# A graph network block on one core: node table first, no barrier at the first pass, one radial piece ahead of the loop and eight inside it, three one-hot buffers

## The reference

```python
x_j = x[src]
v_j = x_j[:, :384].reshape(E, 128, 3)
s_j = silu(x_j[:, 384:] @ W1 + b1) @ W3 + b3
rbf = jnp.sqrt(2.0 / R_CUT) * jnp.sin(n * jnp.pi * r / R_CUT) / r          # n = 1..20
cutoff = 0.5 * (jnp.cos(jnp.pi * r / R_CUT) + 1.0) * (r < R_CUT)
edge_basis = rbf * cutoff @ W2 + b2
s1, s2, s3 = split(s_j * edge_basis)                                        # 128 columns each
v_msg = v_j * s1[:, :, None] + s3[:, :, None] * edge_attr1[:, None, :]
x = x + segment_sum(concatenate([v_msg, s2]), dst)
```

## Time and profile before

| | before |
|---|---|
| device time, three runs | 711.1, 714.84 (median), 719.67 us |
| span of the profiled execution | 711.8 us |
| busy: PE / DVE / ACT / POOL | 505.8 / 537.0 / 389.5 / 370.2 us |
| first gather issued | 144.38 us |
| first and last product of the loop | 154.72 us, 551.50 us (its end) |
| bytes moved by DMA | 139.26 MB, of these 102.91 by gathers |

### The profile page before, as it was taken

The page is one execution under the profiler, slowest core; times in us unless marked ns, Lnnn a source line. Parts: engine busy times, 40 slices in busy tenths (PEclk is TensorE's granted clock), DMA queues, the critical chain, the costliest instruction groups (busy, mean ns, idle before and its releaser), DMA issues.

```text
span 711.8 us, 13058 instructions
## 1 busy us (share of the span) xinstructions
PE 505.8 (71%) x4260; PEld 234.1 (33%) x4269; DVE 537.0 (75%) x1192; ACT 389.5 (55%) x713; POOL 370.2 (52%) x375
## 2 busy tenths in 40 slices
PE   0276430038888888888888888888888286689996
PEld 0232110013333333334433333333333153344443
DVE  8868861029999999999999999999999443354283
ACT  1054331046777777776776777777776364343200
POOL 5004440067777777777777777777773131025300
PEclk9975555559999999999999999999999688689999
DMA  8413777699888888898888888888884400000021
GB/s 277 166 21 99 199 229 222 183 256 306 269 269 272 269 275 270 267 275 268 269 273 269 270 271 271 270 270 269 273 271 149 160 3 0 1 0 1 2 89 56
DMA packets 54193, 139.26 MB, mean 196 GB/s; under 512 B 10366, under 2 KB 21850, under 8 KB 54124
## 3 DMA queue, kind: packets, MB, share of 16 engines
q0 software_dynamic: 25120, 102.91, 46.3%
q1 hardware_dynamic: 23132, 25.80, 12.8%
q10 hardware_dynamic: 5872, 9.68, 4.1%
HBM read 120.47 MB, written 17.54 MB: 194 GB/s over the span
## 4 chain that ended last, share of the span: by engine, by line
DVE 39%; PE 35%; DMA 8%; issue 8%; ACT 3%; SPq 2%; POOL 2%; DVEq 1%; ACTq 1%; POOLq 0%
PE psum L1192 11%; DVE side L929 10%; PE psum L1282 9%; DVE hot L920 5%; DMA part_rows<-side 5%; DVE side L926 4%; PE psum L1157 4%; DVE work L929 3%; DVE work L947 3%; PE psum L1186 3%; PE psum L1251 3%; DVE hot L911 2%; SPq L358 2%; DVE side L916 2%; DMA side<-node_table,src_c 2%
## 5 line engine op out<-in xcount | busy, mean ns | idle before, releaser
L486 POOL DMA_INDIRECT side<-node_table,src_c x234 | 224.4, 959 | 71.3 <-issue 60.4
L604 ACT ACTIVATE side<-key_no,less_key 128x320 bf16<-128x320 f32 x314 | 159.3, 557 | 30.7 <-SPq L384 28.9
L612 ACT ACTIVATE side<-side,one_f 128x640 bf16<-128x640 bf16 x157 | 128.1, 816 | 10.0 <-PE psum L1168 10.0
L1157 PE MATMUL psum<-w2s,radial 123*128 123x384 bf16 x314 | 78.7, 333 | 66.3 <-DVE side L929 43.5
L1186 PE MATMUL psum<-side,hot 128*32 128x512 f32 x468 | 123.1, 605 | 0.5 <-DVE side L929 0.5
L929 DVE TENSOR_TENSOR side<-side,psum 128x768 f32<-128x768 f32 x117 | 110.5, 945 | 0.0
L486 POOL DMA_INDIRECT work<-node_table,src_c x80 | 76.8, 960 | 60.6 <-SPq L384 36.5
L1192 PE MATMUL psum<-side,hot 128*32 128x128 f32 x1404 | 99.4, 277 | 0.0
L926 DVE TENSOR_TENSOR side<-side,psum 128x512 f32<-128x512 f32 x117 | 79.4, 678 | 1.3 <-DMA side<-node_table,src_c 1.3
L1168 PE MATMUL psum<-side 128*128 128x320 bf16 x314 | 70.3, 306 | 0.5 <-ACT side L612 0.5
L1192 PEld LDWEIGHTS psum<-side,hot 128*32 128x32 f32 x1404 | 68.0, 109 | 0.1
(11 more groups left out here) (202 smaller groups left out, 738.0 us busy)
## 6 DMA issues: line engine op xcount, KB each, us to landing
radial<-part_rows SPq DMA_DIRECT2D x36, 270.0 KB
part_rows<-side SPq DMA_DIRECT2D x6, 810.0 KB, 12.7
side<-node_table,src_c POOLq DMA_INDIRECT x234, 4.2
sum_rows<-stage SPq DMA_DIRECT2D x212, 16.0 KB
node_table<-work ACTq DMA_DIRECT2D x10, 320.0 KB, 7.6
sum_rows<-zeros_bf SPq DMA_DIRECT2D x1, 2688.0 KB, 18.8
side<-sum_rows ACTq DMA_DIRECT2D x10, 256.0 KB, 4.7
xw<-in_x ACTq DMA_DIRECT2D x1, 2304.0 KB
```

The costliest lines, as they stand in the source:

```text
L486: g.indirect_dma_start(out=rows[i % SLOT_PAIRS][:, j, :], out_offset=None, in_=node_table, in_offset=bass.IndirectOffsetOnAxis(ap=src_c[:, ...
L604: a.activation(key_off[:, b, j, :], key_no[:, :], ACT.Abs, bias=less_key[:, t:t + 1]).then_inc(L["key_off_made"], 1)
L612: a.activation(key_hot[:, b, :, :], key_off[:, b, :, :], ACT.Relu, bias=one_f[:, :], scale=-1.0).then_inc(L["key_hot_made"], 1)
L1157: last = mm(bank[2 * (i % 2) + j][:, 0:C3], radial[0:RROWS + 3, t * P:(t + 1) * P], w2s[:, :], start=True, stop=True)
```

## The change

1. *Order of the head.* The last quarter of x is loaded first, into a tile `x_in` in `side`; then W1, W3, the rest of x, the zeros for the sums, all on ACT's queue. `filter_of` starts as soon as `hT` is there; it has three PSUM banks, and the table's rows four buffers instead of two. The edge tables are made between the filters. DVE takes the first filter straight from PSUM. Splitting W2 and the biases, constants and the zeroing of the counts are POOL's; edge numbers to floats and `ea_c` are ACT's. `wu2` shares the buffer of `w3` and is loaded after the last filter.
2. *Radial pieces.* Nine pieces of 120x768, one in the head, eight in the loop: piece 1 at pairs 0 to 8, piece `i` from pair `18 * (i - 1) - 8` on. r and the coefficient are kept in float32 and loaded by SP broadcast over 20 rows; `pick` and its matmuls are gone. The steps lie between the pairs of DVE and ACT. The subtractions that POOL did are DVE's. There is one buffer of everything, and it lies in `xw`, so x is loaded there near the loop's end.
3. *Stacks from SBUF.* `part_rows` is gone: SP copies the parts within SBUF into `radial`, and loads r and the coefficient of the next piece behind them.
4. *No barrier.* Each engine enters the first pass when what it needs itself is there. The pass's close is done only if a second pass follows. Semaphores are counted by constants instead of registers.
5. `HOTS` is 3.

The core of the diff:

```diff
-HOTS = 2
+HOTS = 3
-PIECES = 6
-PB = 3
+PIECES = 9
+FILTER_BANKS = 3
+TABLES = 4
...
+        def rc_piece(k, i):
+            piece = rc_rows[k, i * PG:(i + 1) * PG].rearrange("(c f) -> c f", c=CHUNKS)
+            return piece.unsqueeze(0).to_broadcast((N_RBF, CHUNKS, PC))
+
+        def piece_at(i):
+
+            return 0 if i == 1 else PIECE_PAIRS * (i - 1) - 8
+
+        def piece_pairs(step):
+
+            return {piece_at(i) + step: i for i in range(1, PIECES)}
+
+        def stores_before(i):
+
+            return -(-(piece_at(i) + 2) // GP)
...
+            def load_r(i):
+                if i:
+                    sp.wait_ge(S["turn_begun"], i)
+                sp.dma_start(r_in, rc_piece(0, i)).then_inc(S["r_loaded"], 16)
...
+            def load_stack(i):
+                sp.wait_ge(S["lo_made"], i + 1)
+                for q, k in enumerate(STACK):
+                    sp.dma_start(radial[q * N_RBF:(q + 1) * N_RBF, i * PG:(i + 1) * PG].rearrange("p (c f) -> p c f", c=CHUNKS),
+                                 part[:, k, :]).then_inc(stack_in[i], 16)
...
-            sp.sem_inc(S["pass_go"], 1)
-            with sp.Fori(0, rounds_of(sp)) as r:
...
+                    if n in pieces:
+                        load_stack(pieces[n])
+                        if pieces[n] + 1 < PIECES:
+                            load_r(pieces[n] + 1)
+                            load_coef(pieces[n] + 1)
+                    if pieces and n == NG - 4:
+                        load_x()
+
+            store_sums({stores_before(i): i for i in range(1, PIECES)})
...
+            pool.wait_ge(S["edges_taken"], 3)
+            for b in range(TABLES):
+                pool.wait_ge(table_stored[b], 16 * through(NW, b, TABLES))
+            for i in range(PAIRS):
+                gather(i)
...
+            act.wait_ge(S["x_pads"], 1)
+            load_x(C3, D, S["ld_s"])
+            for to, from_ in ((w1[:, :], W1), (b1c[:, :], b1.rearrange("(p a) -> p a", a=1)), (w3[:, :], W3)):
+                a.dma_start(to, from_).then_inc(S["ld_table_weights"], 16)
+            load_x(0, C3, S["ld_v"])
+            act.wait_ge(S["dve_const"], 2)
+            a.dma_start(sum_rows.rearrange("(p b r) c -> p b (r c)", p=P, b=ZB),
+                        zeros_bf[:, :].bitcast(F32).unsqueeze(1).to_broadcast((P, ZB, 256))).then_inc(S["sums_zeroed"], 16)
...
+            sine_at, high_at, middle_at = piece_pairs(3), piece_pairs(5), piece_pairs(7)
...
+            def turns(i):
+                dve.wait_ge(S["r_loaded"], 16 * (i + 1))
+                if i:
+                    dve.wait_ge(S["lo_made"], i)
+                v.tensor_scalar(wave, r_in, harmonic[:, :], None, ALU.mult).then_inc(S["turn_begun"], 1)
+                dve.wait_ge(S["turn_begun"], i + 1)
+                v.tensor_scalar(nearest, wave, MAGIC, MAGIC, ALU.add, ALU.subtract).then_inc(S["turn_near"], 1)
...
+            turns_at, remainder_at, scaled_at = piece_pairs(0), piece_pairs(1), piece_pairs(4)
+            less_high_at, low_at = piece_pairs(6), piece_pairs(8)
...
+            pe.wait_ge(S["table_vec_made"], NW)
+            pe.wait_ge(S["base_taken"], 1)
+            pe.wait_ge(S["bias_rows_set"], 16)
+            pe.wait_ge(S["carry_zeroed"], 1)
+            pe.wait_ge(S["uv_set"], 1)
+            sum_pass()
```

More of the change, by code:

```diff
@@ L362, in _ @@
[L362 to L372 removed]
+            load_stack(0)
@@ new lines, in _ @@
+            then(g.tensor_scalar(lane_k, lane_k, -float(SPAN), None, ALU.mult))
+            then(g.tensor_tensor(lane, lane, lane_k, ALU.add))
+            then(g.tensor_scalar(lane_diff[:, :], node_no[:, 0:SPAN], lane, -1.0, ALU.subtract, ALU.mult))
+            g.tensor_scalar(stack[:, :], lane_diff[:, :], 0.0, None, ALU.is_equal).then_inc(S["pool_const"], 1)
+            pool.wait_ge(S["edges_turned"], 5)
+            pool.wait_ge(S["span_made"], 2)
+            pool.wait_ge(S["r_stored"], 16)
```

713 lines of the change are left out of this document (349 added, 364 removed).

## The result

The changed kernel took **748.2 us** (median of four runs, 744.9 to 757.3) where the kernel before took 715.2 (median of four, 711.1 to 719.7): 1.043 of the time before, 95% interval 1.036 to 1.051. The ratio leaves out the longest execution, 757.3 us, which fell in the chip's slower state. I had forecast 655, in a range of 637 to 680. It is slower by 4% where I had forecast faster.

What follows compares the result with a forecast made beforehand. The prediction took DVE to bound the loop, with DMA close behind. Start 63, loop 427.3 and tail 161.3 summed to 651.6 us; as the median was 3.0 above the profiled run, it forecast 655, range 637 to 680.

Steps and rivals of the forecast that it cites:

- the sum stores behind a piece come late by less than two groups: 0: Loop, SP's queue: the stage holds sum stores delayed behind a piece's transfers, and SP's issues have room; 0 us.
- not faster: Loop rival: every piece's copies come late, pieces 3 to 8 hold DVE as piece 2 does; 721 us, chance 0.04.
- Third buffer, -16.5: Loop: with three one-hot buffers DVE's L911 no longer waits for the pair two back; -16.5 us.
- Pieces' DVE work, +36: Loop: eight radial pieces add 4.5 us each to DVE, in full on the path; +36 us.
- Blocking: Loop rival: DVE's tensor_scalar and POOL exclude each other, 16 instructions at +1.04 us; 672 us, chance 0.07.
- r late at piece 2, +8: Loop, pair 10: DVE waits 3 to 15 us for piece 2's r, issued behind the stack; +8 us.
- Collisions, +3: Loop, DMA: pieces' copies, gathers and sum stores collide at times while DVE stays the bound; +3 us.
- the ten engines, 671: Loop rival, the second case: ten DMA engines become the bound, +17 in place of +3; 671 us, chance 0.21.
- The loop's sum: First product to end of the last: 396.8 - 16.5 + 36 + 8 + 3 = 427.3 us.
- The start, 63: Head: first product at 63 us instead of 154.7, with hT at 18 and base_b taken at 47.3.
- Stack 0 by 59: hidden: Head: stack 0's six copies issue and land by 59 us, beside the chain to the first product.
- Tail, 161.3: From the last product to the end: 160.3 us as before, +1 for the load of x.

Runs made afterwards that it cites:

- e15: The kernel before with three one-hot buffers and one of six gathers left out from pair 8 on: 697.1 us, 0.979 of before.
- e10: The base with two one-hot buffers instead of three: 698.9 us, 0.977 of before.
- e9: The base run a second time, the same kernel as e4: 684.7 us, 0.957 of before.
- e1: The kernel before with a third one-hot buffer, two tiles cut to make room: 725.9 us, 1.013 of before.
- the base: The changed kernel with the loop pieces' transfers issued from ACT's queue instead of SP's: 686.1 us (e4) and 684.7 us (e9).
- e4: The changed kernel with the loop pieces' transfers on ACT's queue instead of SP's, first run: 686.1 us, 0.957 of before.
- e2: The changed kernel without the 64 transfers of the loop's pieces, their computing steps kept: 682.0 us, 0.953 of before.
- e7: The base with the copy of ones cut in two, 54 packets ahead of stack 0 and the rest behind: 0.916 of before, on another chip.
- e5: The base with two one-hot buffers, on another chip: 0.932 of before.
- e8: The kernel before with the same two tiles cut as in e1 but two one-hot buffers, on another chip: 1.0015 of before.
- e6: The base with the gathers held until stack 0 has landed, on another chip: 0.913 of before.

## Why the forecast was wrong

- **SP's queue, "the sum stores behind a piece come late by less than two groups: 0".** This step failed. Moving the transfers off that queue gives 62 us by time, 66.3 in the loop of the profiled runs, and is enough to make the kernel 4% faster than before. Some 50 of the 66 are this term, forecast at 0; some 16 are the stop for r, forecast at 8. I had the bytes and their own rate (10 us), and took SP's waits of 128 us as room in its queue. But a sum store landed behind what was issued ahead of it on its queue, and that took 27 us where gathers filled the same engines. The stores took 18 to 26 us; `stage` covers 7 to 9. The rival "not faster", at 721, had the right kind (a stop at every piece from 2 on, the clock falling, as it did to 0.50 here), but the wrong waiter: r for the next piece, for which 22 us stand ready, where the stores have 7. I gave it 0.04.
- **Third buffer, -16.5.** Near in size where POOL has room (e15: -20); that e10 against e9 gives -14 is partly luck, as two thirds of the waits it takes away are of another kind. I took before's loop for DVE's alone; it was also the gathers', 7.5 of 7.56 us. "More isn't there since DVE then never stops" is false in e1, where DVE stands 27.7 us for gathers.
- **Pieces' DVE work, +36.** Right: the tensor_scalars took 0.62 and 0.56 us, the four tensor_tensor 0.94 to 0.95, 0.87 from start to start, 4.6 in sum (forecast 4.5). "Blocking" with tensor_scalar over 1 us did not come in the loop; the one of piece 0, at 33.1 us in the head, took 1.36.
- **r late at piece 2, +8.** In after DVE stood 17.2 us for it; three later stops of 1.8 to 3.3 us fall under the waits for sum stores. In the base it isn't among the waits.
- **Collisions, +3, and the ten engines, 671.** The transfers cost 3 to 4 us by time and 3.2 and 0.8 in the loop (e4 and e9 against e2). The second case did not happen.
- **The loop's sum.** The base's loop, without the queue's fault, took 429.6 us where 427.3 were forecast. That is luck in part: the 8 for r were not needed, and something in no term, most likely the long gathers, took their place. With no transfers at all (e2) the loop took 428.8, where the terms without 8 and 3 say 416.3.
- **The start, 63.** The chain to base_b is right to 0.1 us, but by luck: hT was ready at 13.5 us and not 18, since nothing held ACT, and then PE waited 7.21 us for `bias_parts`, which no term had. "Stack 0 by 59: hidden" failed: PE had it at 87.3, for I had left the copy of ones out of the count, though it stands right ahead of the stack on the queue.
- **Tail, 161.3.** 164.2: behind the load of x the last sum stores are 3 us later than I had allowed.

## What to carry to other kernels

Before a bulk transfer is put on a queue, list what is issued behind it there and how long each of these can wait; price the wait by the time the bulk takes beside the other queues' traffic, not by its bytes alone. A small transfer that someone waits for belongs on another queue than a bulk one that nobody needs soon: the same bytes cost 65 us on one and 3 to 4 on the other (15 when spread over the first). And an engine that issues software gathers is full when its issues are back to back; add the gaps to its busy time before calling another engine the bound.

## What the runs showed of the hardware that I had not expected

- Issuing a gather of 128 rows holds POOL 0.95 us and the next starts 0.30 later; when it starts under DVE's SBUF-only tensor_tensors, it takes up to 1.61 (e1). In before, where the two engines have almost the same pace, 1 of 268 gathers starts there; with one wait of DVE taken away it is 66 of 253.
- Issuing a transfer is not of fixed cost. A stack copy took from 0.76 us (e7) to 8.48 (the first behind the ones), a weight load 32.80 behind 432 packets for three engines. The issuing engine stands meanwhile, with all that is behind it.
- A copy into 3 rows ran at a share of 0.16 and 30 GB/s. The Trainium skill (DMA: Bandwidth & Descriptors, section "Why a DMA increments its semaphore by 16 and not by 1") gives it three engines, 0.19; the row agrees.
- The four runs e5 to e8 were on a chip on which the kernel before takes 801 us, 12% more, with the clock at 0.99 and the DMA share lower, 0.77 (e8, 172 to 300 us). Its gathers are not issued back to back:

```profile
299.19 1.15 POOL L486 DMA_INDIRECT side<-node_table,src_c  x1 [1.10 <-remote]
300.64 0.95 POOL L486 DMA_INDIRECT side<-node_table,src_c  x1 [0.30 <-issue]
302.32 1.15 POOL L486 DMA_INDIRECT side<-node_table,src_c  x1 [0.74 <-remote]
```

  18 pairs take 55 us there in e6, e7 and e8 alike, and 57.7 in e5. The profile doesn't name who releases them, and this stays open.
